# A four-layer graph network on one core: three one-source operations of DVE in the attention loop get a second source tensor

## The reference

```
z  = einsum('nd,hdf->nhf', h, W)                 # per node, 4 heads x 64
e  = leaky_relu(es[src] + ed[dst], 0.01)         # one logit per edge and head
e  = where(e == 0.0, -1000.0, e)
m  = segment_max(e, dst)
ex = exp(e - m[dst])
out = segment_sum(ex / segment_sum(ex, dst)[dst] * z[src], dst)
```

## Time and profile before

| | us |
|---|---|
| median of 3 runs | 2205.11 (2187.52 to 2212.55) |
| the profiled execution | 2198.86 |
| its span | 2197.0 |
| PE busy in the span | 1904.5 |
| DVE busy | 1288.8 |
| POOL busy | 734.0 |
| ACT busy | 443.9 |

### The profile page before, as it was taken

One profiled execution on the slowest core, in us unless ns is written; L12 is line 12 of the kernel. 1 busy time (PEld: TensorE's weight loads), 2 busy tenths in 40 slices (PEclk: granted clock), 3 DMA queues, 4 the chain that ended last, 5 costly groups with the idle time before them and its releaser, 6 DMA issues.

```text
span 2197.0 us, 38284 instructions
## 1 busy us (share of the span) xinstructions
PE 1904.5 (87%) x13533; PEld 1656.8 (75%) x13533; DVE 1288.8 (59%) x2915; ACT 443.9 (20%) x999; POOL 734.0 (33%) x567
## 2 busy tenths in 40 slices
PE   6679999999999888888648788887899887799998
PEld 5478888888888777777537777777788775588887
DVE  9577776777677111111358887888888886511111
ACT  0412212222221000000022222232332223300000
POOL 0122122112211100000168888888888870000000
PEclk9989999999999999999855555555555555599999
DMA  7111121121112443333033333333333332044441
GB/s 177 39 62 64 66 90 64 63 93 64 63 78 102 158 130 111 117 130 118 22 71 86 79 83 78 85 84 81 86 85 86 84 76 90 30 141 170 169 167 42
DMA packets 110199, 202.38 MB, mean 92 GB/s; under 512 B 70372, under 2 KB 87061, under 8 KB 100483
## 3 DMA queue, kind: packets, MB, share of 16 engines
q1 hardware_dynamic: 54851, 141.62, 18.4%
q0 software_dynamic: 55232, 59.15, 11.3%
HBM read 152.00 MB, written 53.36 MB: 93 GB/s over the span
## 4 chain that ended last, share of the span: by engine, by line
PE 74%; DVE 7%; POOL 6%; issue 5%; DMA 4%; ACT 3%; DVEq 1%; POOLq 0%; SPq 0%; ACTq 0%
PE bank L1216 25%; PE bank L1282 12%; PE bank L1152 10%; PE bank L1160 10%; POOL ring L446 6%; PE bank L1149 4%; DMA ring<-attention_rows,work 3%; PE bank L1273 3%; PE bank L1178 2%; PE bank L1346 2%; PE bank L1256 2%; DMA work<-in_src 2%; PE bank L1169 1%; PE bank L1224 1%; DVE work L920 1%
## 5 line engine op out<-in xcount | busy, mean ns | idle before, releaser
L446 POOL DMA_INDIRECT ring<-attention_rows,work x425 | 569.0, 1339 | 144.6 <-issue 129.7
L1282 PE MATMUL bank<-work,ring 125*65 125x48 f32 x3400 | 393.9, 302 | 0.0
L1282 PEld LDWEIGHTS bank<-work,ring 125*65 125x65 f32 x3400 | 386.5, 224 | 8.3
L1152 PE MATMUL bank<-work 128*128 128x100 bf16 x2400 | 304.0, 273 | 0.0
L1216 PE MATMUL bank<-big,ring 128*128 128x256 f32 x1250 | 279.8, 386 | 1.4 <-DVE x_sb L814 1.4
L1216 PE MATMUL bank<-big 128*128 128x256 f32 x1250 | 278.0, 384 | 0.0
L1216 PEld LDWEIGHTS bank<-big,ring 128*128 128x128 f32 x1250 | 241.1, 194 | 35.9 <-DVE x_sb L814 2.2
L1216 PEld LDWEIGHTS bank<-big 128*128 128x128 f32 x1250 | 240.1, 193 | 33.4
L1152 PEld LDWEIGHTS bank<-work 128*128 128x128 bf16 x2400 | 242.6, 117 | 0.0
L1160 PE MATMUL bank<-big 128*128 128x256 bf16 x1875 | 212.2, 275 | 14.6 <-ACT big L489 14.6
L1149 PE MATMUL bank<-work 128*128 128x100 bf16 x800 | 218.2, 273 | 6.9 <-DVE work L776 4.6
(11 more groups left out here) (204 smaller groups left out, 2268.4 us busy)
## 6 DMA issues: line engine op xcount, KB each, us to landing
adjacency<-big SPq DMA_DIRECT2D x25, 1600.0 KB, 5.2
ring<-adjacency SPq DMA_DIRECT2D x25, 1600.0 KB, 7.4
big<-adjacency SPq DMA_DIRECT2D x25, 1600.0 KB, 7.3
ring<-attention_rows,work POOLq DMA_INDIRECT x425, 4.2
edge_rows<-edge_list SPq DMA_DIRECT2D x1, 4983.0 KB
x_sb<-in_x SPq DMA_DIRECT2D x1, 3072.0 KB
out_x<-xnT SPq DMA_DIRECT2D x24, 128.0 KB, 4.3
attention_rows<-ring SPq DMA_DIRECT2D x13, 135.0 KB, 2.3
```

The lines of the kernel that those rows point to most:

```text
L446: G.indirect_dma_start(out=rows[0:EP, s, c, 0:ZG], out_offset=None, in_=ztab[:, :], in_offset=bass.IndirectOffsetOnAxis(ap=idx[:, s, c:c + ...
L1152: ins = mm(w_banks[b][:, 0:NT * QUAD * PAN].rearrange("p (b d) -> p b d", b=NT)[:, :, cols], lo[:, g, :, k], wtd[:, j, g, :, k].rearrange( ...
L1282: ins = mm(sum_banks[three(s)][0:FH, h * WIN:(h + 1) * WIN], rows[0:EP, s, c, h * FH:(h + 1) * FH], prob[:, s % 2, c, h * WIN:(h + 1) * WI ...
```

## The change

The three operations get a second source tensor and compute the same values. `relative` takes the window's first node as a tensor repeated along the row. `logits_zero` multiplies with a new constant tile `neg` that holds -1000 and is repeated over the heads. `keep_max` takes the maximum of `new` with itself instead of with -1e30. A memset for `neg` is added in the set-up.

```
+        neg = sb("neg", [P, KC])
...
             V.memset(far[:], -3 * BIG)
+            V.memset(neg[:], NEG)
...
                 def relative(k):
                     s, g = k % SLOTS, q * SLOTS + k
                     dve.wait_ge(y["slot_free"], number(k) + 1)
-                    V.tensor_scalar(rel[:, s, :], dstf[:, bass.ds(g, 1), :].rearrange("p a k -> p (a k)"),
-                                    base_f[0:EP, bass.ds(g, 1)], None, ALU.subtract).then_inc(y["relok"], 1)
+                    V.tensor_tensor(rel[:, s, :], dstf[:, bass.ds(g, 1), :].rearrange("p a k -> p (a k)"),
+                                    base_f[0:EP, bass.ds(g, 1)].to_broadcast([EP, KC]), ALU.subtract).then_inc(y["relok"], 1)
...
                 def logits_zero(k):
                     dve.wait_ge(y["lg"], 5 * number(k) + 8)
-                    V.tensor_scalar(lg[:, 2], lg[:, 1], 0.0, NEG, ALU.is_equal, ALU.mult).then_inc(y["lg"], 1)
+                    V.scalar_tensor_tensor(out=lg[:, 2], in0=lg[:, 1], scalar=0.0,
+                                           in1=neg[0:EP, :].unsqueeze(2).to_broadcast([EP, KC, H]), op0=ALU.is_equal,
+                                           op1=ALU.mult).then_inc(y["lg"], 1)
...
                 def keep_max(k):
                     dve.wait_ge(y["dm_ready"], number(k) + 1)
-                    V.tensor_scalar(runmax[:, :, bass.ds(window_base(k), WIN)], new, -BIG, None,
-                                    ALU.max).then_inc(y["rm_ready"], 1)
+                    V.tensor_tensor(runmax[:, :, bass.ds(window_base(k), WIN)], new, new, ALU.max).then_inc(y["rm_ready"], 1)
```

## The result

| | before | after |
|---|---|---|
| median, us | 2203.85 (2187.52 to 2212.55, 4 runs) | 2239.52 (2237.65 to 2242.29, 4 runs) |
| the profiled execution | 2198.86 | 2242.29 |
| its span | 2197.0 | 2240.4 |
| mean of a gather, ns | 1339 | 1440 |

The change makes the kernel slower: 1.0188 times the time before, 95% interval 1.0151 to 1.0226. I had forecast 2167 us, faster. The direction was wrong, and the time lies outside the range.

A forecast was written before the change was run, and what follows sets the result against it. POOL's gapless gathers were taken to bound layer 2's loop, with PE's ring close behind. 2198.86 minus 24.7 (PE's ring becomes the bound) minus 7 (fast-clock spells) gave 2167 us; range 2145 to 2185.

The forecast's parts named there:

- POOL sets the loop's length, by gapless gathers: Layer 2's loop: 425 gathers with 0.30 us gaps fill 698.2 us, 8.21 us a group; POOL never waits.
- The one-source TENSOR_SCALARs stretch the gathers: Layer 2's loop: gathers run long where keep_max, relative or logits_zero lies; two-source forms would remove all 54.3 us.
- a rival: No effect: long gathers are POOL's own, or any DVE operation there makes them; 2199 to 2205 us, chance 0.12.
- The 54.3 us of stretches: Layer 2's gathers: busy 569.05 us, of which 514.7 are work at the 1.211 us median and 54.3 are extra length.
- The effect is mutual: DVE beside gathers: one-source L920 takes 163 ns at best, 401 in the median; two-source L931 stays at 1142 to 1170.
- PE's ring of 7.80 us with 8.42 at the turn: Closed chain of PE and DVE in layer 2's loop; each fifth round 8.42; becomes the bound at 673.5 us, gain 24.7.
- The spells' 7 us: Some seven spells of PE at 2.4 GHz: a group takes 6.74 us against 7.80, 1.0 us gained in each.
- keep_max's 8.3 us hidden: DVE in layer 2's loop: the two-source form costs 0.10 us x 85, covered by waits for rows and PE; taken as 0.
- the others' prices: On DVE: logits_zero's new form 168 ns against 352; relative 0.05 us saved or lost, 4.5 us over 85 groups.
- The slower rival: Layer 2's loop: keep_max's place is the mechanism, its longer new form holds POOL off; 35.7 us more, 2234.6, chance 0.06.
- open rhythm: Layer 2's loop: L920 short, gather around L975 2.04 us, L911 waits 1.88 us for rows, PE's round 8.51 us.
- the 180 gathers: Gathers beside which only two-source DVE operations start; ten over 1.24 us; taken as evidence against the no-effect and slower cases.

The follow-up runs named there:

- the last PSUM kernel: Kernel before with DVE operands (new maximum, group values, relative's result, three logits parts) in a free PSUM bank, plus two-source logits_zero: 2173.63 us, 0.9885.
- the first PSUM kernel: Kernel before with the new maximum, its group values, relative's result and three logits parts in a free PSUM bank: 2174.42 us, 0.9915.
- the reordered kernel: Kernel with those operands in PSUM, and max_diagonal moved right behind group_max, ahead of logits_leaky, rescale and logits_zero: 2230.08 us, 1.0144.
- the second experiment: Kernel before with only relative and keep_max in two-source form, logits_zero as it was, neg and its memset kept: 2190.03 us, 0.9993.

## Why the prediction was wrong, point by point

**POOL sets the loop's length, by gapless gathers: right.** After the change too: 42.9 us of gathers and 43.4 us of span.

**"The one-source TENSOR_SCALARs stretch the gathers": the step that failed.** I had sorted the gathers by what *begins* while they run. keep_max begins in every gather that shifted holds, since it follows shifted directly on DVE, and relative follows masked in the same way. They were companions of the cause, relative always and keep_max for the most part: it held on in 20 of its 82 gathers, 6 of the 44.0 us, and its two-source form does so too. That an L975 of 0.24 us goes with a gather 0.83 us longer was in the prediction as an argument for a rival; it was the better argument. What holds a gather is a two-source operation that runs at its start. The 54.3 us of stretches were there, but the change could remove none of them: after it they are 611.9 - 425 x 1.211 = 97.2 us.

**"The effect is mutual": half right.** A one-source L920 does wait for the gather, but in the traces no one-source operation begins a hold; the one-source keep_max carried on some that shifted had begun, by 0.30 us. I read L920's wait as a cost of 0.08 us on PE's ring, when its worth was the place of masked: 2% of the time.

**PE's ring of 7.80 us with 8.42 at the turn: right, in the kernel that has short gathers.** The most frequent rounds of the last PSUM kernel are 7.80 and 7.79 us (50 of 84), with 8.41 to 8.44 at nine of its 16 turns. My term for it was 24.7 us; the loop of the first PSUM kernel is 698.2 - 672.5 = 25.7 us shorter than before.

**The spells' 7 us: wrong.** The PSUM kernel's loop is 672.5 us against 673.5 with no spell counted, though it had 44 us at the upper clock level, in eight spells. The rounds begun in them take 6.66 to 9.14 us, 7.69 in the mean, against the usual 7.79: two are as short as the 6.74 that I had estimated, but in the longer spells DVE's group_max starts 2.2 to 3.3 us behind the recorded end of PE's transpose. In one of them PE's transposed maximum is done at 1507.71, and DVE, which waits from 1509.36 on, is let go at 1510.42 (the semaphore event is dated 1510.39):

```profile
1507.29 0.42 PE L1269 MATMUL bank<-ident,work 125*96 125x125 f32 x2
...
1510.42 0.42 DVE L948 TENSOR_REDUCE bank<-bank 96x2 f32<-96x250 f32 x1 [1.06 <-remote]
```

Why is open; it looks like the late releases of the reordered kernel, which come outside of spells too.

**keep_max's 8.3 us hidden, the others' prices: right**, by the second experiment and the rows above.

**The slower rival** gave 2234.6 us, open rhythm for good and a mean gather above 1.339 us; 2239.5 and 1.440 came. Its picture of the end state was right, but it hung on keep_max being 0.10 us longer, which by itself, together with relative's new form, does nothing (0.9993). I gave it 0.06 because it, too, was measured against the 180 gathers.

**What I should have seen in the trace of before:** the gather of 1.21 us in the earlier trace rows at 1407.46 starts under L939, a reduction with one source, and L965 and L899 begin only after its start. Beside it has the gather of 1408.98, which starts under L970. A table by what runs at the start needs no run of another kernel.

## What to carry to other kernels

When one engine's instruction is longer at times, sort its occurrences by what was running when it started, not only by what began beside it: a follower in a fixed order is always there and need not be guilty. Then check the lengths too: here they showed that one follower had a part after all. A wait that looks like a waste may be what ties two engines' rhythms to each other, so before it is removed, ask which two operations it has kept apart. Here the remedy was in the operands: with one of two sources in PSUM in the long operations, the form of logits_zero no longer mattered.

## What the runs showed of the hardware that I had not expected

- An indirect DMA on POOL of 1.21 us is held by a DVE operation with two SBUF sources that runs at about 0.1 us after its start. In the twelve traces of this case the first operation of a hold started at the latest 0.09 us behind the gather. The gather then lasts to the operation's end plus 1.08 us: up to 1.1 us longer under one masked. It is not held at all by an L931 of 1.15 us that began 0.08 us behind it.
- What follows without a gap can hold on, in one-source form too (L975, by 0.30 us, in 20 of 82 cases before the change). max_change, one_hots, shifted and keep_max in a row made a gather of 3020 ns.
- A one-source operation of 125x20, SBUF to SBUF, took 161 to 604 ns beside gathers; with its result in PSUM it took 171 in the mean.
- The same wait is worth nothing or 2%, depending on whether anybody waits for the one who waits (1.0227 against 1.0007).
- DVE, ACT and SP went on up to 3 to 4 us after the matmul records end, in some thirty groups of one kernel (1.0144) and in few of its neighbour. The semaphore events are late with them, so this is more than missing records; but the ends of matmuls are modelled in these profiles, and how much of the lag is real, and its cause, stay open.
